# Graph kernel on one core: edge batches of 14 tiles instead of 8, compared in a triangle, with the counts taken on ScalarE

## What is computed

```python
row, col = edge_index                      # src, dst of 50000 edges
ew  = clip(abs(edge_weight), 1e-6, None)
deg = segment_sum(ew, col) + 1.0;  dis = rsqrt(deg)
# graph convolution, twice:
agg = segment_sum((dis[row]*ew*dis[col])[:, None] * (h @ W)[row], col)
h   = relu(layernorm(agg + dis*dis*(h @ W) + b)) + h
# gated graph network, five times:
agg = segment_sum((h @ weight[i])[src] * edge_weight[:, None], dst)
h   = gru_cell(agg, h, w_ih, w_hh, b_ih, b_hh)
```

## Time and profile before

| what | value |
|---|---|
| median of 3 runs | 3995.4 us (3994.84 to 3998.62) |
| the profiled execution | 3991.95 us, span 3990.0 us, mean granted clock 0.928 |
| PE busy | 3090.3 us (77%) |
| DVE, ACT, POOL busy | 2332.0, 1249.5, 1448.0 us |
| POOL, `plane_a` DMAs (L491) | 392, 652.7 us busy |
| POOL, `plane_w` DMAs (L497) | 392, 662.0 us busy |

### The profile page before, as it was taken

One profiled execution on the slowest core, in us unless ns is written; L12 is line 12 of the kernel. 1 busy time (PEld: TensorE's weight loads), 2 busy tenths in 40 slices (PEclk: granted clock), 3 DMA queues, 4 the chain that ended last, 5 costly groups with the idle time before them and its releaser, 6 DMA issues.

```text
span 3990.0 us, 54476 instructions
## 1 busy us (share of the span) xinstructions
PE 3090.3 (77%) x17984; PEld 2742.4 (69%) x17985; DVE 2332.0 (58%) x5541; ACT 1249.5 (31%) x2259; POOL 1448.0 (36%) x922
## 2 busy tenths in 40 slices
PE   2455453200799994999959999999999999999698
PEld 2454442100688884888848988998998998899565
DVE  7999993511587786655574554545555555555333
ACT  0000000110344552333334444444444444444122
POOL 1577888877767676677710000000000000000000
PEclk9999997655899996999979999999999999999699
DMA  9876334576667666344254433433343333432100
GB/s 397 263 220 177 42 42 74 108 213 164 159 173 196 175 164 180 82 133 129 36 175 154 138 116 124 128 126 124 127 131 119 127 127 116 135 122 90 57 11 22
DMA packets 381089, 538.33 MB, mean 135 GB/s; under 512 B 126115, under 2 KB 283978, under 8 KB 377482
## 3 DMA queue, kind: packets, MB, share of 16 engines
q1 hardware_dynamic: 251076, 487.82, 36.1%
q0 software_dynamic: 119088, 19.33, 8.6%
q10 hardware_dynamic: 10774, 29.17, 2.0%
HBM read 398.99 MB, written 137.24 MB: 134 GB/s over the span
## 4 chain that ended last, share of the span: by engine, by line
PE 43%; DVE 5%; ACT 1%; issue 1%; DMA 1%; SPq 0%; ACTq 0%; POOL 0%; DVEq 0%
PE bank L597 38%; PE bank L874 2%; PE bank L868 1%; DVE ring_lo L1623 1%; PE bank L776 1%; PE bank L845 1%; DVE gates_sb L1649 0%; ACT ring_hi L1074 0%; DVE res L1685 0%; DVE gates_sb L1648 0%; DVE res_b L1735 0%; DVE fo L1789 0%; DVE xT L1650 0%; DMA yg_end<-chosen 0%; DVE v_lo L1680 0%
## 5 line engine op out<-in xcount | busy, mean ns | idle before, releaser
L491 POOL DMA_INDIRECT plane_a<-pair,slot x392 | 652.7, 1665 | 282.5 <-issue 118.8
L497 POOL DMA_INDIRECT plane_w<-pair,slot x392 | 662.0, 1689 | 232.0 <-issue 120.7
L597 PE MATMUL bank<-ring_hi,h_hi 128*128 128x448 f32 x1750 | 651.6, 372 | 58.8 <-DVE ring_lo L1623 53.4
L1623 DVE TENSOR_TENSOR ring_lo<-ring_lo,ring_hi 128x448 fp32r<-128x448 f32 x875 | 521.9, 621 | 218.4 <-ACT ring_hi L1074 218.1
L597 PE MATMUL bank<-ring_lo,h_hi 128*128 128x448 f32 x1750 | 642.5, 367 | 0.0
L597 PE MATMUL bank<-ring_hi,h_lo 128*128 128x448 f32 x1750 | 642.3, 367 | 0.0
L1074 ACT ACTIVATE ring_hi<-ring_lo 128x448 fp32r<-128x448 f32 x875 | 497.2, 576 | 380.5 <-PE bank L597 373.9
L545 POOL DMA_DIRECT2D v_lo<-gru_v x5 | 3.6, 723 | 1381.8 <-PE bank L597 1307.5
L597 PE MATMUL bank<-gring_hi,hs_hi 128*128 128x512 f32 (+2 forms) x700 | 261.9, 374 | 276.4 <-DVE gring_lo L1338 276.4
L597 PEld LDWEIGHTS bank<-ring_hi,h_hi 128*128 128x128 f32 x1750 | 331.2, 189 | 86.3 <-DVE h_lo L1690 47.2
L570 PE MATMUL bank<-parts,eq 128*128 (+1 forms) x3136 | 132.3, 170 | 318.8 <-DVE hit_hi L1286 318.7
(11 more groups left out here) (325 smaller groups left out, 5912.2 us busy)
## 6 DMA issues: line engine op xcount, KB each, us to landing
ring_lo<-plane_w SPq DMA_DIRECT2D x175, 1120.0 KB, 5.4
gring_lo<-plane_a SPq DMA_DIRECT2D x50, 1280.0 KB, 5.9
plane_a<-nat SPq DMA_DIRECT2D x25, 1600.0 KB, 45.3
plane_w<-nat SPq DMA_DIRECT2D x100, 400.0 KB
w_hl<-w_split SPq DMA_DIRECT2D x16, 2048.0 KB
keyrow<-key_rows ACTq DMA_DIRECT2D x49, 512.0 KB, 4.0
part_in<-in_L_ffn_W SPq DMA_DIRECT2D x16, 1024.0 KB, 10.1
w_split<-part_hi SPq DMA_DIRECT2D x16, 1024.0 KB, 4.4
```

The costliest lines, as they stand in the source:

```text
L491: g_.indirect_dma_start(out=plane, out_offset=bass.IndirectOffsetOnAxis(slot[:, t:t + 1], 0), in_=pair[:, k, t:t + 1], in_offset=None, com ...
L497: g_.indirect_dma_start(out=plane_w, out_offset=bass.IndirectOffsetOnAxis(slot[:, n:n + 1], 0), in_=pair[:, 0, n:n + 1], in_offset=None, c ...
L597: last = mm(ps, lhs[x], rhs[y], start=start and n == 0, stop=stop and n == 2)
L1623: V.tensor_tensor(ring_lo[:, t, :], ring_lo[:, t, :].bitcast(FP32), ring_hi[:, t % HS, :].bitcast(FP32), ALU.subtract).then_inc(lo_rdy, 1)
```

## The change

It touches the edge stage and the three pacing tables.
- Batches have 14 tiles (`G` = 14, `NB` = 28), and the keys of a batch have 2 buffers.
- DVE compares tile q only with the tiles 0 to q (1 to 14 blocks of 128 keys, 105 blocks per batch in place of 196). Matmul block (q, g) is there for q of g or above: 105 products per batch. The `own` instructions are gone.
- Earlier equal keys are counted in two ways. For the tile itself, a power of two per partition (falling with the partition's number) stands as a seventh column, and DVE asks whether the sum is above 2.5 times its own power. For earlier tiles, ACT runs 13 Copy instructions with an accumulating output over 1 to 13 blocks of `eq` (new function `count_before`), ahead of its copy of the sums.
- DVE's next comparison waits for the counts two batches back (`counts`), and so does `place` for its own batch.
- `plane_w` is filled 13 pieces per batch, its tiles are slipped in from batch 9 on (19 instead of 32), 252 tiles instead of 256 are issued ahead of the experts, and the parts wait for batch 14 + 3n/4 in place of 30 + n.
- Some tiles in SBUF share room that had been separate.

```diff
-G = 8
-KB = 4
+G = 14
+KB = 2
 NB = ET // G
-W1 = 32
-FB, FIRST_W = 8, 17
-BP, P0 = 30, 4
+UP = G * (G + 1) // 2
+W1 = 18
+FB, FIRST_W = 13, 9
+BP, P0 = 14, 4
...
-                sp.wait_ge(scat_a, 16 * G * (BP + n))
+                sp.wait_ge(scat_a, 16 * G * (BP + n * 3 // 4))
...
                 for g in range(G):
-                    for q in range(G):
-                        parts = (parts1 if q < g else parts0)[:, bass.ds(n * G + q, 1), :].rearrange("p a k -> p (a k)")
-                        mm(ps_sum[c][:, g, :], eq[:, c, q, g * EP:(g + 1) * EP], parts, start=(q == 0), stop=(q == G - 1))
+                    parts = lambda q, cols: parts0[:, bass.ds(n * G + q, 1), 0:cols].rearrange("p a k -> p (a k)")
+                    mm(ps_sum[c][:, g, :], eq_row(c, g, g, g + 1), parts(g, 8), start=True, stop=(g == G - 1))
+                    for q in range(g + 1, G):
+                        mm(ps_sum[c][:, g, 0:6], eq_row(c, q, g, g + 1), parts(q, 6), start=False, stop=(q == G - 1))
...
+            def count_before(n, c):
+                act.wait_ge(compared, n + 1 + KB)
+                act.wait_ge(placed, n + 1)
+                for q in range(1, G):
+                    act.wait_ge(passed_on, n * (G - 1) + q)
+                    A(passed[:, q % 2, 0:q * EP], eq_row(c, q, 0, q), ACT.Copy, accum_out=before_n[:, c, q:q + 1]).then_inc(passed_on, 1)
+                act.wait_ge(passed_on, (n + 1) * (G - 1) + 2)
+                act.sem_inc(counts, 1)
+
             def take_sums(n, c):
+                count_before(n, c)
                 act.wait_ge(summed, n + 3)
...
-                for g in range(G):
-                    V.tensor_scalar(eq[:, c, g, :], keyrow[:, b, :], at(key, g), None, ALU.is_equal)
-                for g in range(G):
-                    V.scalar_tensor_tensor(own[:, c, g, :], keyrow[:, b, g * EP:(g + 1) * EP], at(key, g), before[:, :], ALU.is_equal, ALU.mult, accum_out=own_n[:, c, g:g + 1])
+                v.wait_ge(counts, n + 1)
+                for q in range(G):
+                    V.tensor_scalar(eq_row(c, q, 0, q + 1), keyrow[b][:, 0:(q + 1) * EP], at(key, q), None, ALU.is_equal)
...
             def place(n, c):
                 v.wait_ge(sums_out, n + 3)
+                v.wait_ge(counts, n + 3)
...
-                link(V.tensor_tensor(earlier[:, c, :], sums[:, c, :, 6], own_n[:, c, :], ALU.add))
+                link(V.scalar_tensor_tensor(earlier[:, c, :], sums[:, c, :, 6], beyond[:, 0:1], before_n[:, c, :], ALU.is_gt, ALU.add))
```

More of the change, by code:

```diff
@@ L163, in build @@
         lo_i, hi_i, spare_i = (early[:, m, :].bitcast(I32) for m in (5, 6, 7))
-        srci = sb("srci", [EP, ET], I32); dsti = sb("dsti", [EP, ET], I32); w = sb("w", [EP, ET])
+        w = sb("w", [EP, ET])
         wabs = sb("wabs", [EP, ET]); key = sb("key", [EP, ET])
-        dlo = sb("dlo", [EP, ET]); dhi = sb("dhi", [EP, ET]); to_spare = sb("to_spare", [EP, ET])
-        parts0 = sb("parts0", [EP, ET, 8], BF16); parts1 = sb("parts1", [EP, ET, 8], BF16)
-        before = sb("before", [EP, EP])
-        keyT = sb("keyT", [ET // 4, 4, EP])
+        dlo, dhi = srcf, dstf
+        to_spare = sb("to_spare", [EP, ET])
+        parts0 = sb("parts0", [EP, ET, 8], BF16)
+        order_i = sb("order_i", [EP, 1], I32); order = sb("order", [EP, 1]); beyond = sb("beyond", [EP, 1])
         hit_lo = sb("hit_lo", [EP, 2, G, 128]); hit_hi = sb("hit_hi", [EP, 2, G, NT])
-        own = sb("own", [EP, 2, G, EP], BF16); own_n = sb("own_n", [EP, 2, G])
+        passed = sb("passed", [EP, 2, (G - 1) * EP], BF16); before_n = sb("before_n", [EP, 2, G])
         sums = sb("sums", [EP, 2, G, 8]); half = sb("half", [EP, 2, G, 2])
@@ L174, in build @@
         scope.append(ExitStack())
-        keyrow = sb("keyrow", [EP, KB, G * EP])
-        eq = sb("eq", [EP, 2, G, G * EP], BF16)
+        eq = sb("eq", [EP, 2, UP * EP], BF16)
+        eq_row = lambda c, q, lo, hi: eq[:, c, (q * (q + 1) // 2 + lo) * EP:(q * (q + 1) // 2 + hi) * EP]
         scope.pop().close()
@@ L181, in build @@
         spare = xT[:, :, :].rearrange("p k n -> p (k n)")
+        keyrow = (front[:, 0:G * EP], spare[:, KD * NP - G * EP:KD * NP])
+        keyT = eq[0:ET // 4, 0, 0:8 * EP].bitcast(FP32).rearrange("t (c p) -> t c p", c=4)
+        srci, dsti = (eq[:, 1, 2 * ET * n:2 * ET * (n + 1)].bitcast(I32) for n in range(2))
         wt_sb = spare[:, 0:LAYERS * KD * D].rearrange("p (i k f) -> p i k f", i=LAYERS, k=KD)
@@ L259, in build @@
         keyrow_in = [sem(f"keyrow_in{b}") for b in range(KB)]
-        compared = sem("compared"); summed = sem("summed"); sums_out = sem("sums_out"); placed = sem("placed")
+        compared = sem("compared"); counts = sem("counts"); passed_on = sem("passed_on"); summed = sem("summed"); sums_out = sem("sums_out"); placed = sem("placed")
         scat_a = sem("scat_a"); scat_w = sem("scat_w"); deg_done = sem("deg_done")
@@ L467, in _ @@
             g_ = nc.gpsimd
-            g_.memset(srci[:, :], NP - 1).then_inc(padded, 1)
-            g_.memset(dsti[:, :], NP).then_inc(padded, 1)
+            g_.memset(srci, NP - 1).then_inc(padded, 1)
+            g_.memset(dsti, NP).then_inc(padded, 1)
             g_.memset(w[:, :], 0.0).then_inc(padded, 1)
@@ L474, in _ @@
             g_.memset(ident[:, :], 0.0).then_inc(consts, 1)
-            g_.memset(before[:, :], 1.0).then_inc(consts, 1)
+            g_.iota(order_i[:, :], [[0, 1]], base=187, channel_multiplier=-1).then_inc(consts, 1)
             g_.memset(below[:, :], 1.0).then_inc(consts, 1)
@@ L482, in _ @@
             g_.affine_select(out=ident[:, :], in_=ident[:, :], compare_op=ALU.not_equal, fill=1.0, base=0, pattern=[[-1, 128]], channel_multiplier=1).then_inc(consts, 1)
-            g_.affine_select(out=before[:, :], in_=before[:, :], compare_op=ALU.is_gt, fill=0.0, base=0, pattern=[[-1, EP]], channel_multiplier=1).then_inc(consts, 1)
             g_.affine_select(out=below[:, :], in_=below[:, :], compare_op=ALU.is_gt, fill=0.0, base=0, pattern=[[1, 128]], channel_multiplier=-1).then_inc(consts, 1)
@@ L891, in _ @@
             act.sem_inc(sums_out, 2)
+            act.sem_inc(counts, 2)
+            act.sem_inc(passed_on, 2)
             act.wait_ge(keyT_ps, 1)
@@ L1259, in _ @@
             go(V.tensor_scalar(finite, wbits, FLT_MAX, None, ALU.is_le))
-            v.wait_ge(consts, 10)
+            v.wait_ge(consts, 9)
+            link(V.tensor_scalar(order[:, :].bitcast(I32), order_i[:, :], 23, None, ALU.logical_shift_left))
+            go(V.tensor_copy(parts0[:, :, 6], order[:, :].to_broadcast([EP, ET])))
+            go(V.tensor_scalar(beyond[:, :], order[:, :], 2.5, None, ALU.mult))
             link(V.tensor_copy(to_spare[:, :], spare_i))
@@ L1299, in _ @@
             compare(0, 0, 0)
-            with ch.loop(0, NB // KB, 2 * KB) as i:
+            LOOPED = NB // KB - 1
+            with ch.loop(0, LOOPED, 2 * KB) as i:
                 for b in range(KB):
@@ L1303, in _ @@
                     place(KB * i + b, b % 2)
-            place(NB - 1, (NB - 1) % 2)
+            for n in range(KB * LOOPED, NB):
+                if n + 1 < NB:
+                    compare(n + 1, (n + 1) % KB, (n + 1) // KB)
+                place(n, n % 2)
             def rest_of_part(n):
```

21 lines of the change are left out of this document (9 added, 12 removed).

## The result

The changed kernel takes **3972.59 us** (median of 4 runs, 3963.17 to 3972.98); before, on the same chip, 3996.38 us (3994.84 to 3998.62). The ratio is 0.9934, 95% interval 0.9917 to 0.9952: faster by some 24 us where 47.7 were forecast (a ratio of 3947.7 / 3995.4 = 0.988), and just above the range of 3930 to 3970. The two profiled executions are 19.1 us apart.

What follows compares the result with a forecast made beforehand. POOL's plane_a tiles were taken to bound the convolution's start, and POOL the experts' stage. −44.0 us there and −3.7 us in the experts sum to −47.7 us, giving 3947.7 us, range 3930 to 3970.

Steps and rivals of the forecast that it cites:

- DVE's hold on POOL: POOL tiles waiting on DVE comparisons: shorter total and longer instructions cancel, 0 us; upper gain bound −26 us.
- rival 3: Longer holds: 71 POOL tiles each wait out a full comparison, +61 us, time 4009; chance 0.03.
- Tiles of plane_a: POOL's plane_a stage: 13 slipped tiles go behind and 8 boundaries fewer, −44.0 us, end near 970 us.
- The rest of the batch: DVE, PE and ACT work per batch takes 16 to 19 us, faster than POOL's 30.7; cost 0.
- Fill and parts: Zero fill of plane_w and the parts' loads and stores finish early enough; cost 0.
- plane_w under the convolution: 233 POOL tiles and 16 boundaries take 535 us; POOL idles some 26 us before the experts; cost 0.
- rival 1: Given back later: denser plane_w tiles slow the convolution, experts pay for 4 more; time 3963; chance 0.12.
- Experts: Experts' stage on POOL: 4 tiles more (+7.4 us), boundaries 17 to 10 (−11.1 us), together −3.7 us; bounds −11 to +7.
- Rival 2: Less hold: removing DVE's own instructions frees POOL of 7 us, time 3941; chance 0.15.
- a first ring load behind 1000 us: SP's first load from plane_a for the convolution's ring; later than 1000 us would make the prediction wrong.

Runs made afterwards that it cites:

- e13: Changed kernel with each batch's fast comparisons split into two runs (rows 0 to 9, rows 10 to 13), half of the hits after each; 3995.05 us, ratio 1.0009.
- e5: Changed kernel with every equality comparison written as an add to zeros in PSUM followed by the compare; 3968.13 us, ratio 0.9929.
- e11: Kernel before the change with its eight 1024-element comparisons per batch in the form that adds to zeros in PSUM; 4129.83 us.
- e12: Changed kernel with only comparison rows 7 to 13 (77 of 105 blocks) in the form that adds to zeros in PSUM; 3924.43 us, ratio 0.9825.
- e8: The changed kernel itself, unaltered, run again on another chip; 3964.94 us, ratio 0.9933.

## Why the prediction was wrong

The step that failed is **DVE's hold on POOL**: "The two cancel. The bounds are the whole hold (−26 us) and full-length waits (rival 3); I take 0". It weighed the total time of the comparisons (264 to 250 us) against the mean wait for the end of one, and took each wait to end with one instruction. The runs showed that a waiting tile can be passed over by several comparisons in a row (e13: four). The hold went from 0.14 us a tile to between 0.30 and 0.35 in this stretch. Over the first 126 tiles the means differ by 0.211 × 126 = 26.6 us, of which the four long tiles make some 18. The issue gaps, with the late ones of 7.66 and 5.21 us among them, differ by 49.5 − 126 × 42.9 / 136 = 9.8 us. Less 3 us for a wait of 2.96 us at 404.61 us in the old stretch, which the forecast's 2.03 us per tile held and the new stretch doesn't have, these are the 33.4 us between 307.0 and 273.6. How much of the gaps is DVE's is not shown: the three longest sum to 14.8 us here and to 9.4 us in e5. That the hold exists, and that the comparisons make it, was in the text and was right; that it hangs on their form is what e5 showed, which took away all of it, and e11 sized it before.

Point by point:
- *Tiles of plane_a, −44.0 us*: came to −13.9 at the ring load. Boundaries cost 2.19 us (2.23) and the 285 tiles of the second stretch 1.98 us (2.00). The stage took 872.4 us instead of 843.6, 33.4 more in the first stretch and 4.6 less in the second, and began 1.4 us later than before.
- *The rest of the batch, 0*: right. DVE needed 16.0 us for a batch (15.6), ACT's 364 counts took 339.9 us (12.1 a batch) and their reads 68.2 us (2.4 a batch), as worked out without the waits, the longest count 1575 ns (about 1.6 us), and POOL never waited for a place. The last batch was placed at 506.44 us, inside 500 to 600.
- *Fill and parts, 0*: right here; the parts were over at 925 us, 75 ahead of the ring load. e12 and e5 show where they come to bind.
- *plane_w under the convolution, 0*: POOL idled 24.66 us ahead of the first gather (26). The stretch grew by 2.0 us, under rival 1's 5.
- *Experts, −3.7*: measured −8.9. The 140 tiles cost (221.4 + 41.1) / 140 = 1.88 us each (1.86), but the boundary waits fell from 26.9 to 8.6 us instead of 15.8. Inside the bounds of −11 to +7.
- *Rival 3* came nearest (longer holds, mean above 1.9 us in the profiled execution, 1.86 in e8's) and had a chance of 0.03. Its mechanism was another one, though: 71 tiles that each wait out one full instruction, 61 us. Here 4 tiles waited through several and the rest lost little more than before, about 33 us with the gaps, so the kernel stayed faster than before. *Rival 2* (`own` out, 7 us less hold) is ruled out: e11 kept `own`, and its first 136 tiles have a mean of 1554 ns, so `own` held less than 1 us in all.
- The text said that a first ring load behind 1000 us would make it wrong. It came at 1001.41 (991.13 in e8).
